# Product-key layers: head 2's pair sums move to TensorE, head 0's are shared by GpSimd and ScalarE

## The reference

```
xn = rmsnorm(x, norm_w)
q = (xn @ w_q.T).reshape(b, t, H, 2, DK)              # H = 8 heads
sim1, sim2 = q halves against 32 keys each            # (b, t, H, 32)
s1, i1 = top_k(sim1, 8);  s2, i2 = top_k(sim2, 8)
fs, pk = top_k(s1[..., :, None] + s2[..., None, :], 8)
hidden = gelu(xn . expert_down[fi]) * relu(fs)        # fi: the 8 chosen of 1024 experts
out = sum over heads and chosen experts of hidden * expert_up[fi]
```

## Time and profile before

| | us |
|---|---|
| median of three runs | 2678.5 |
| the profiled execution | 2683.22 |
| its span | 2681.5 |
| stage 5's tiles, from first to last instruction | about 473 |
| stage 7's tiles | about 471 |

### The profile page before, as it was taken

The page is one execution under the profiler, slowest core; times in us unless marked ns, Lnnn a source line. Parts: engine busy times, 40 slices in busy tenths (PEclk is TensorE's granted clock), DMA queues, the critical chain, the costliest instruction groups (busy, mean ns, idle before and its releaser), DMA issues. The chain is left out here.

```text
span 2681.5 us, 59371 instructions
## 1 busy us (share of the span) xinstructions
PE 2094.4 (78%) x17450; PEld 1739.1 (65%) x17451; DVE 2254.2 (84%) x5549; ACT 1864.0 (70%) x4275; POOL 1617.8 (60%) x1472
## 2 busy tenths in 40 slices
PE   4748888879599999693488877888888447888888
PEld 2336666658488888573466656777777326777777
DVE  6489999875588888656888857999999788999998
ACT  3579999756555555463255547999999349999997
POOL 0069999717300000274555547999999209999997
PEclk9869999989899999796799998999999769999999
DMA  2013333241200000111100000000000000000000
GB/s 60 3 48 97 97 96 97 72 143 52 64 1 0 0 0 1 48 52 42 41 2 0 0 1 1 0 0 0 0 0 0 1 0 1 4 8 4 4 4 8
DMA packets 67879, 70.65 MB, mean 26 GB/s; under 512 B 10408, under 2 KB 46464, under 8 KB 67648
## 3 DMA queue, kind: packets, MB, share of 16 engines
q1 hardware_dynamic: 61632, 57.56, 7.5%
q0 software_dynamic: 4992, 10.23, 1.4%
q10 hardware_dynamic: 1120, 1.22, 0.2%
...
## 5 line engine op out<-in xcount | busy, mean ns | idle before, releaser
L1899 POOL TENSOR_TENSOR k5a_psums<-k5a_sims 128x1024 f32<-128x1024 f32 x224 | 421.7, 1914 | 16.2 <-DVE k5a_w L2107 12.0
L1899 POOL TENSOR_TENSOR k7a_psums<-k7a_sims 128x1024 f32<-128x1024 f32 x224 | 421.7, 1915 | 12.9 <-DVE k7a_w L2107 8.7
L994 POOL TENSOR_TENSOR mc_hc<-mc_h,mc_cs 128x512 f32<-128x512 f32 x256 | 328.0, 1297 | 32.7 <-DVE mc_h L961 17.3
L1964 PE MATMUL k5a_pw<-g_ident,k5a_w 128*128 128x128 f32 x2048 | 265.6, 277 | 70.4 <-DVE k5a_hid L2115 45.9
L1964 PE MATMUL k7a_pw<-g_ident,k7a_w 128*128 128x128 f32 x2048 | 262.0, 276 | 70.1 <-DVE k7a_hid L2115 45.9
L1964 PEld LDWEIGHTS k5a_pw<-g_ident,k5a_w 128*128 128x128 f32 x2048 | 226.8, 141 | 113.7 <-DVE k5a_w L2107 52.7
L961 DVE TENSOR_TENSOR_SCAN mc_h<-mc_dA,mc_inj 128x512 f32<-128x512 f32 x256 | 298.5, 1200 | 2.3 <-PE mc_inj L850 1.8
L1964 PEld LDWEIGHTS k7a_pw<-g_ident,k7a_w 128*128 128x128 f32 x2048 | 227.3, 141 | 109.4 <-issue 63.8
L2107 DVE SCALAR_TENSOR_TENSOR k7a_w<-k7a_psums,k7a_best,k7a_lift 128x1024 f32<-128x1024 f32 x224 | 279.5, 1272 | 0.5 <-ACT k7a_lift L2035 0.3
L2107 DVE SCALAR_TENSOR_TENSOR k5a_w<-k5a_psums,k5a_best,k5a_lift 128x1024 f32<-128x1024 f32 x224 | 279.1, 1270 | 0.5 <-ACT k5a_lift L2035 0.3
L2035 ACT ACTIVATE k7a_lift<-k7a_psums 128x1024 f32<-128x1024 f32 x224 | 229.2, 1023 | 37.5 <-DVE k7a_w L2107 33.2
...
## 6 DMA issues: line engine op xcount, KB each, us to landing
mc_cs<-c_rows SPq DMA_DIRECT2D x128, 256.0 KB, 3.1
...
e_zs<-token_rows,e_token POOLq DMA_INDIRECT x78, 2.6
token_out<-e_ys,e_token POOLq DMA_INDIRECT x78, 2.3
```

Source lines behind the costliest of these rows:

```text
L994: nc.gpsimd.tensor_tensor(hc[:, q % RH, :], h_[:, q % RB, :], cs[:, S % RC, :], ALU.mult).then_inc(outs, 1)
L1899: nc.gpsimd.tensor_tensor(psums[:, h - 1, :, :], rows_of(p, h), s2, ALU.add).then_inc(pooled, 1)
L1964: ins = nc.tensor.matmul(pw[:, j, :], w[:, h % WR, j * P:(j + 1) * P], env.ident[:, :], start=(h == 0 and j % 4 == 0), stop=(h == HD - 1 a ...
```

## The change

The pair sums of head 2 (`HP`) are no longer formed by POOL but by PE. A score is split into three bf16 parts: ACT copies the score to bf16 (`leading`), DVE subtracts (`leave`), ACT copies the rest to bf16 (`second`), DVE subtracts again (`trail`). PE transposes the parts into `pmix` (`turn`, two matmuls), ACT copies them to `simT` (`carry`), and PE multiplies them by a table of ones (`pair`, four bf16 matmuls of 512 columns), which gives head 2's 1024 pair sums in `lift`. For this head `raise_` copies from `lift` to the SBUF tile `esum`, scaled by 1 + 2^-22, and `weigh` compares `esum` and multiplies by `lift`. The table `ones` is built by POOL in `k5f` and `k7f` with three copies.

Of head 0's pair sums POOL makes rows 0 to 19 and ACT the other 12 (before: DVE 16, ACT 16). DVE's `form` is gone. On PE, `sim(t+2)` moves from ahead of `sum_up(t, 6)` to behind it.

```diff
+        PARTS = 3
+        ones = sb("ones", [PARTS * K, 3, K // 2, K], BF16)
+        placed = sem("placed")
+
+        def place(pool):
+            for q in range(2):
+                nc.gpsimd.tensor_copy(ones[:, q, :, :], env.sel[:, q * K // 2:(q + 1) * K // 2, 0:K]).then_inc(placed, 1)
+            cols = env.sel[:, :, 0:1].rearrange("p j o -> p o j").broadcast_to([PARTS * K, K // 2, K])
+            nc.gpsimd.tensor_copy(ones[:, 2, :, :], cols).then_inc(placed, 1)
+            pool.wait_ge(placed, 3)
+
+        begin(nc, env, tag + "f", (1.0, 1e-6, 0.0, 1.0), True, ZT, g[:, 0:1], weights, len(weights), on_pool=place)
...
-            NP, WR, LR = HD - 1, 4, 2
-            dsum, psums = sb("dsum", [P, K, K]), sb("psums", [P, NP, K, K])
+            HP, WR, LR = 2, 4, 2
+            ABOVE = 1.0 + 2.0 ** -22
+            POOLED = [h for h in range(HD) if h != HP]
+            NP = len(POOLED)
+            psums, esum = sb("psums", [P, NP, K, K]), sb("esum", [P, NE])
+            parts, rest = sb("parts", [P, 2, PARTS, K], BF16), sb("rest", [P, 2, K])
+            simT = sb("simT", [PARTS * K, 2, P], BF16)
...
-            SHARE, GROUPS = K // 2, 4
+            SHARE, GROUPS = 20, 4
...
-                src = dsum[:, :, :] if h == 0 else psums[:, h - 1, :, :]
-                return src.rearrange("p i j -> p (i j)")
+                if h == HP:
+                    return esum[:, :]
+                return psums[:, POOLED.index(h), :, :].rearrange("p i j -> p (i j)")
...
+                    rows = K if h else SHARE
+                    s2 = sims[:, p, h, 1, :].rearrange("p (o j) -> p o j", o=1).broadcast_to([P, rows, K])
+                    nc.gpsimd.tensor_tensor(psums[:, POOLED.index(h), 0:rows, :], rows_of(p, h)[:, 0:rows, :], s2,
+                                            ALU.add).then_inc(pooled, 1)
...
                 def sim(t, p):
 
                     need(pe, copied, t + 1)
-                    need(pe, dsummed, t)
+                    need(pe, entered, t)
                     need(pe, added, t - 2)
...
+                def turn(t):
+
+                    need(pe, low, t + 1)
+                    need(pe, added, t - 1)
+                    for z in range(2):
+                        ins = nc.tensor.matmul(pmix[0:PARTS * K, z * P:(z + 1) * P], parts[:, z, :, :].rearrange("p a k -> p (a k)"),
+                                               env.identb[:, :], start=True, stop=True)
+                    ins.then_inc(split, 1)
+
+                def pair(t):
+
+                    need(pe, entered, t + 1)
+                    need(pe, weighed, t * HD + HP + 1 - LR)
+                    for q in range(2):
+                        for z, e in enumerate((q, 2)):
+                            ins = nc.tensor.matmul(lift[:, HP % LR, q * 512:(q + 1) * 512], simT[:, z, :],
+                                                   ones[:, e, :, :].rearrange("p i j -> p (i j)"), start=(z == 0), stop=(z == 1))
+                    ins.then_inc(paired, 1)
...
+                        if not final:
+                            turn(t + 1)
+                        sum_up(t, 6)
                         if not last:
                             sim(t + 2, p)
-                        sum_up(t, 6)
                         sum_up(t, 7)
...
                     need(act, scored, t + 1)
                     need(act, pooled, (t - 1) * NP)
-                    need(act, dsummed, t - 1)
+                    need(act, left, t - 1)
                     need(act, topped, t - 1)
...
+                def leading(t, p):
+
+                    need(act, s_in, t + 1)
+                    need(act, split, t)
+                    nc.scalar.copy(parts[:, :, 0, :], sims[:, p, HP, :, :]).then_inc(high, 1)
+
+                def second(t):
+
+                    need(act, left, t + 1)
+                    nc.scalar.copy(parts[:, :, 1, :], rest[:, :, :]).then_inc(middle, 1)
+
+                def carry(t):
+
+                    need(act, split, t + 1)
+                    need(act, paired, t)
+                    nc.scalar.copy(simT[:, :, :].rearrange("p z c -> p (z c)"), pmix[0:PARTS * K, 0:2 * P]).then_inc(entered, 1)
...
-                    for i in range(SHARE + q * SHARE // GROUPS, SHARE + (q + 1) * SHARE // GROUPS):
-                        ins = nc.scalar.activation(dsum[:, i, :], sims[:, p, 0, 1, :], ACT.Identity,
+                    for i in range(SHARE + q * (K - SHARE) // GROUPS, SHARE + (q + 1) * (K - SHARE) // GROUPS):
+                        ins = nc.scalar.activation(psums[:, 0, i, :], sims[:, p, 0, 1, :], ACT.Identity,
                                                    bias=sims[:, p, 0, 0, i:i + 1])
...
+                    if h == HP:
+                        need(act, paired, t + 1)
+                        need(act, weighed, (t - 1) * HD + HP + 1)
+                        nc.scalar.activation(esum[:, :], lift[:, h % LR, :], ACT.Identity, scale=ABOVE).then_inc(lifted, 1)
+                        return
                     if h == 0:
                         need(act, asummed, GROUPS * (t + 1))
-                        need(act, dsummed, t + 1)
-                    else:
-                        need(act, pooled, t * NP + h)
+                    need(act, pooled, t * NP + POOLED.index(h) + 1)
                     need(act, weighed, t * HD + h + 1 - LR)
...
                         if not final:
                             enter(t + 1, 1 - p)
+                            leading(t + 1, 1 - p)
                         raise_(t, 1)
                         if not final:
                             sums(t + 1, 1 - p, 0)
                         raise_(t, 2)
                         if not final:
+                            second(t + 1)
                             sums(t + 1, 1 - p, 1)
...
                         if not final:
+                            carry(t + 1)
                             gate(t + 1, 1 - p, 1)
...
-                def form(t, p):
-
-                    need(dve, s_in, t + 1)
-                    need(dve, weighed, (t - 1) * HD + 1)
-                    s2 = pmix[:, K:2 * K].rearrange("p (o j) -> p o j", o=1).broadcast_to([P, SHARE, K])
-                    nc.vector.tensor_tensor(dsum[:, 0:SHARE, :], rows_of(p, 0)[:, 0:SHARE, :], s2, ALU.add).then_inc(dsummed, 1)
+                def leave(t, p):
+
+                    need(dve, high, t + 1)
+                    need(dve, middle, t)
+                    nc.vector.tensor_tensor(rest[:, :, :], sims[:, p, HP, :, :], parts[:, :, 0, :], ALU.subtract).then_inc(left, 1)
+
+                def trail(t):
+
+                    need(dve, middle, t + 1)
+                    need(dve, split, t)
+                    nc.vector.tensor_tensor(parts[:, :, 2, :], rest[:, :, :], parts[:, :, 1, :], ALU.subtract).then_inc(low, 1)
...
                         if not final:
                             top8(t + 1, 1 - p)
+                            leave(t + 1, 1 - p)
                         weigh(t, p, 2)
+                        weigh(t, p, 3)
                         if not final:
-                            form(t + 1, 1 - p)
-                        weigh(t, p, 3)
+                            trail(t + 1)
```

More of the change, by code:

```diff
@@ L1875, in product_keys @@
             pw, phd, pmix = ps("pw", [P, J, P]), ps("phd", [P, J // 2, P]), ps("pmix", [P, 512])
[L1876 removed]
+            SHARE, GROUPS = 20, 4
             floored, asummed, stored = sem("floored"), sem("asummed"), sem("stored")
[L1878 removed]
+            high, left, middle, low, split, entered, paired = (sem(x) for x in (
+                "high", "left", "middle", "low", "split", "entered", "paired"))
+            copied, scored, s_in, pooled, topped, crossed, ranked, lifted, weighed, summed, hidden, gelud, \
                 mixed, made, added, measured = (sem(x) for x in (
[L1880 removed]
+                    "copied", "scored", "sin", "pooled", "topped", "crossed", "ranked", "lifted", "weighed",
                     "summed", "hidden", "gelud", "mixed", "made", "added", "measured"))
@@ L1913, in tile_sums @@
                 def tile_sums(t, p):
+                    form(t, p, 0)
                     form(t, p, 1)
                     cross(t)
-                    for h in range(2, HD):
+                    for h in POOLED[2:]:
                         form(t, p, h)
@@ L1950, in out @@
                     need(pe, mixed, t + 1)
-                    need(pe, dsummed, ahead)
+                    need(pe, s_in, ahead)
                     need(pe, added, t)
@@ L1972, in body @@
                         begun, final = first and p == 0, last and p == 1
+                        pair(t)
                         sum_up(t, 0)
@@ L1992, in _ @@
                 hide(0, 1)
+                turn(0)
                 sim(1, 1)
@@ L2068, in _ @@
                 enter(0, 0)
+                leading(0, 0)
+                second(0)
                 for q in range(GROUPS):
@@ L2072, in _ @@
                 gate(0, 0, 1)
+                carry(0)
```

(3 more changed lines are left out.)

5 lines of the change are left out of this document (removed).

## The result

The changed kernel takes 2795.1 us (median of four runs, 2792.6 to 2796.1), the kernel before 2679.5 in the same comparison: a ratio of 1.0427, interval 1.0411 to 1.0442. The forecast was 2780 us. The profiled execution has a span of 2793.9 us, 112.4 more than before.

A forecast was written before the change was run, and what follows sets the result against it. DVE was taken to set the turn, with POOL nearly full; turns of +1.80 us (stage 5) and +1.46 (stage 7), 31 of each, add 101 us to the profiled 2683.2, and 4.7 off gives 2780 us, range 2720 to 2835.

The forecast's parts named there:

- step 1: ACT's `second` delays the raises of heads 3 and 4: DVE weighs them 0.82 and 0.28 us late per turn.
- step 2: PE's `turn` and ACT's `carry` make head 0 late on DVE: 0.22 us in stage 5, 0.72 in stage 7.
- step 3: PE's score matmul `sim` behind `sum_up(6)` makes `finish` late: 0.53 us in stage 5, 0.03 in stage 7.
- step 4: DVE's `leave`, with two SBUF inputs, is held until POOL's sums of head 1 end: 0.46 us more per turn.
- Rival A: The shared SBUF ports do not hold `leave`; only step 1, step 2 and step 3 cost: 73 us, 2751 us; chance 0.25.
- lower bound of step 4: `leave` not held beside POOL's sums: 0 us, from a first-layer operation that took its plain 1.23 us.
- this row: Rows 8, first layer: a DVE operation took its plain 1.23 us beside POOL's 2.36, read as no hold.
- Rival B: DVE's `trail` is also held, by POOL's sums of head 3: 1.7 us per turn, 105 us more, 2885 us; chance 0.12.
- Rival C: Only one of two chains decides; if score matmul and `carry` find places, step 1 remains: 48 us, 2726 us; chance 0.10.
- D: Faster: the full engines DVE and POOL get less work; each turn falls by 0.33 us, 20 us, 2658 us; chance 0.05.

## Why the prediction was right

It was right in sign and mechanism, and 15 us short. By its terms, per turn (a late start is the idle time plus the 0.09 of lost overlap):

| term | forecast, stage 5 / 7 | measured |
|---|---|---|
| head 3 late (step 1) | 0.82 | 0.77 / 0.77 |
| head 4 late (step 1) | 0.28 | 0.26 / 0.26 |
| head 0 late (step 2) | 0.22 / 0.72 | 0.12 / 0.62 |
| `finish` late (step 3) | 0.53 / 0.03 | 0.59 / 0.11 |
| `leave` held (step 4) | 0.46 / 0.46 | 0.45 / 0.66 |
| turn | 16.20 / 15.75 | 16.09 / 15.81 |

Head 0 in stage 5 is read from three weighings in 3.78 us, where 2 x 1.19 + 1.28 = 3.66 would do; `finish` in stage 7 starts 1.30 behind head 0, where 1.19 would do. In stage 7 step 4 was 0.20 too small, because POOL, back to back there, begins head 1's sums 0.29 us behind the end of that head's weighing and not 0.09. That its turn still came out within 0.06 us is in part luck: the three late heads were over-estimated by 0.05, 0.02 and 0.10.

Step 1 is shown by the later `second`, step 4 by three kernels; `leave` from PSUM is worth 39 us against the 28.5 (62 x 0.46) charged for it. Rival A (no hold) had 0.25 and is refuted.

A and the lower bound of step 4 rested on the earlier trace rows, and this row was misread. The code of the first layer says so:

```
            one, l = ps("one", [P, H, CH]), ps("l", [P, 2, H, CH])
...
                    link(nc.vector.scalar_tensor_tensor(one[:, :, :], one[:, :, :], -1.0, e_of(n), ALU.add, ALU.subtract))
```

`ps` makes a PSUM tile, `sb` one in SBUF. So L787 reads `one` from PSUM and only `du` from SBUF: it is a case like `leave` from PSUM and speaks for step 4, not against it. The 0.46 was taken as the nearer of two rows that disagree; they agree.

Rival B (`trail` held too) did not come: 0.22 us at the median and 0.37 at most, and POOL began 0.16 behind it. Rival C was half right in a way I had not written: in stage 5 TensorE's chain (step 3) alone decides when `finish` starts, in stage 7 the chains of steps 2 and 3 end within about 0.1 us of each other, so that taking away step 2 alone gives nothing; the 6 us that this run (2801.0) lost on top go with the misplaced `carry`, 0.41 us ahead of head 6 in stage 7. Both steps taken away give 10 us as long as `leave` is held. Their price alone, free of the hold, was not measured by itself. D came true only with an edit for every step, one for the start and one of TensorE's order.

The step that was mis-sized is the last term of the sum: the first and last tiles and the three table copies, left at nothing with 0 to 8 us for the range. From the stage's start to the first `finish` the changed kernel loses 7.4 and 6.1 us, of which the forecast had the first tile's turn, 3.3: so 10 us. What stands there bare is the new chain: `leave` held for 1.70 us, `second` behind it, the row sums, `turn`, `carry`. In stage 5 the lower clock adds to it (0.5 us at the first score matmul alone); stage 7 loses its 6.1 us without that first part. How the 10 us divide between the chain and the clock was not separated. The copies cost 2.2 us in `k5f` (20.85 us from L139 to the stage's start, 18.64 before), 1.75 of them the three held subtractions, and 1.6 up to the start of stage 7. Together 14 us; with the 31 turns 1 us under the forecast's share of them (30 that prepare a tile, 97.8) and the part ahead of `k5f` 1.5 shorter in this execution, that is 101 + 14 - 2.5 = 112.5, the measured 112.4.
